# Folding the last quarter of W1 on the vector engine instead of the tensor engine, in a quaternion-conditioned feed-forward kernel

## The reference

```
xf = ifft(fft(x_quat, over tokens) * gate).real      # gate: one number a lane, so xf = x_quat * gate
q_l, q_r = cond / |cond|, q_right / |q_right|        # per lane (64 lanes)
z  = hamilton(q_l, hamilton(xf, conj(q_r)))          # cond and x: component by component, per lane
p  = softmax(z @ Wr.T)[:, 7]                         # 8 experts, the last one's probability
h  = gelu(z @ W1[7] + b1[7])                         # 256 -> 1024
out = x + (h @ W2[7] + b2[7]) * p                    # 1024 -> 256
```

## Time and profile before

| | |
|---|---|
| median of 3 runs | 105.12 us (105.01 to 106.14) |
| the profiled execution | 105.81 us, of which its span 104.0 us |
| granted TensorE clock | 1.0 (mean) |
| busy: TensorE, its loader | 100.2 us (96%), 84.9 us (82%) |
| busy: VectorE, ScalarE, GpSimd | 67.0 us (64%), 50.0 us (48%), 25.6 us (25%) |
| DMA | 8.38 MB, mean 81 GB/s |

### The profile page before, as it was taken

How to read it: one execution, slowest core, us unless ns; L and a number is a source line. 1 busy time by engine, 2 the same in 40 slices (tenths; PEclk the granted TensorE clock), 3 DMA queues, 4 the chain that set the end, 5 groups by cost and what they waited for, 6 DMA issues and landing times.

```text
span 104.0 us, 1512 instructions
## 1 busy us (share of the span) xinstructions
PE 100.2 (96%) x568; PEld 84.9 (82%) x568; DVE 67.0 (64%) x145; ACT 50.0 (48%) x83; POOL 25.6 (25%) x16
## 2 busy tenths in 40 slices
PE   7899999999999999999999999999999999999990
PEld 7779978888888888888888888888888878888980
DVE  1579689888274999298225996272494962378451
ACT  1466794544442484484414534944424544442700
POOL 3300000029999300000000000069998000000000
PEclk9999999999999999999999999999999999999999
DMA  3989990260004132450500050000005040000005
GB/s 67 319 266 343 261 121 0 50 135 22 0 3 158 44 115 93 94 111 0 202 0 0 0 208 0 0 0 0 0 0 202 6 202 0 0 0 0 0 7 195
DMA packets 10870, 8.38 MB, mean 81 GB/s; under 512 B 7920, under 2 KB 8816, under 8 KB 10864
## 3 DMA queue, kind: packets, MB, share of 16 engines
q1 hardware_dynamic: 10144, 7.51, 25.0%
q10 hardware_dynamic: 720, 0.79, 2.2%
HBM read 6.20 MB, written 2.10 MB: 80 GB/s over the span
## 4 chain that ended last, share of the span: by engine, by line
PE 93%; DMA 2%; DVE 2%; DVEq 0%; issue 0%
PE pre L690 40%; PE acc L697 26%; PE acc L705 15%; PE pre L654 3%; PE acc L606 2%; PE lT_bank L643 2%; DMA quats<-in_small 2%; PE acc L625 2%; PE acc L701 1%; PE acc L699 1%; DVE y L513 1%; PE lT_bank L625 1%; PE acc L616 0%; DVEq L73 0%; DVE R L390 0%
## 5 line engine op out<-in xcount | busy, mean ns | idle before, releaser
L341 ACT ACTIVATE h_hi<-pre,quats 128x512 fp32r<-128x512 f32 x32 | 22.1, 692 | 43.7 <-PE pre L690 41.8
L479 DVE TENSOR_TENSOR h_lo<-h_all,h_hi 128x512 fp32r<-128x512 f32 x32 | 21.8, 689 | 20.3 <-ACT h_all L343 20.1
L697 PE MATMUL acc<-w_parts,h_hi 128*128 128x512 f32 x116 | 32.4, 392 | 0.0
L697 PEld LDWEIGHTS acc<-w_parts,h_hi 128*128 128x128 f32 x116 | 21.5, 188 | 4.7 <-DVE w_lo L455 0.3
L690 PE MATMUL pre<-xT_hi,w_hi 128*128 128x512 f32 x60 | 24.0, 400 | 0.0
L690 PE MATMUL pre<-xT_lo,w_hi 128*128 128x512 f32 x60 | 23.6, 394 | 0.0
L705 PE MATMUL acc<-w_parts,h_lo 128*128 128x256 f32 x128 | 23.0, 282 | 0.0
L288 POOL TENSOR_TENSOR exps<-e_const,shifted 128x32 f32<-128x32 f32 x4 | 22.2, 5578 | 0.2
L705 PEld LDWEIGHTS acc<-w_parts,h_lo 128*128 128x128 f32 x128 | 20.0, 189 | 2.6 <-DVE h_lo L479 0.7
L343 ACT ACTIVATE h_all<-pre,quats 128x512 f32<-128x512 f32 x32 | 21.9, 684 | 0.0
L690 PE MATMUL pre<-xT_hi,w_lo 128*128 128x512 f32 x60 | 18.7, 392 | 0.0
(11 more groups left out here) (71 smaller groups left out, 61.2 us busy)
## 6 DMA issues: line engine op xcount, KB each, us to landing
x_sq<-in_x SPq DMA_DIRECT2D x12, 128.0 KB, 3.7
x_in<-in_x SPq DMA_DIRECT2D x3, 512.0 KB, 3.2
out<-y SPq DMA_DIRECT2D x3, 512.0 KB, 2.7
w<-in_W SPq DMA_DIRECT2D x4, 256.0 KB, 4.4
x_in<-in_x SPq DMA_DIRECT2D x2, 256.0 KB, 4.6
w_rest<-in_W_rest SPq DMA_DIRECT2D x2, 256.0 KB, 3.4
w_first<-in_W_first ACTq DMA_DIRECT2D x2, 132.0 KB, 2.8
x_sq<-in_x SPq DMA_DIRECT2D x4, 64.0 KB, 3.4
```

The costliest lines, as they stand in the source:

```text
L341: nc.scalar.activation(h_hi[:, s, :], pre_bank(b, f)[:, :], ACT.Gelu, bias=b1_cols[:, f:f + 1]).then_inc(h_hi_ready, 1)
L479: nc.vector.tensor_tensor(h_lo[:, s, :], h_all[:, s, :], h_hi[:, s, :].bitcast(F32), ALU.subtract).then_inc(h_lo_ready, 1)
L697: nc.tensor.matmul(acc[j][:, :], rows, w2_parts[:, f, :, :], start=(f == 0), stop=False)
```

## The change

TensorE no longer folds piece 3. The host gives the unfolded piece as before; the SP queue loads its four component groups of 32 rows one by one, and each goes to all four groups of 32 partitions (`w1_last`, four loads of 256 KB written). GpSimd computes the coefficients of M by column (`column_M`) from a new small input `columns` in five instructions. VectorE sums the four groups: `scale_last_w1` multiplies the first by its coefficient, `add_last_w1(o)` multiplies group o and adds it. Each is one instruction per half. ScalarE writes the high part (`last_w1_high`) behind its splits of x after f = 4, VectorE the low part (`last_w1_low`) behind the logits. The split of W2 piece 2 moves from after low_hidden 3 to behind that. In the SP queue the pieces 2 and 3 of W2, b2 and the second half of the first x move behind the squares of block 1.

```diff
@@ loads on the SP queue
-            for i in range(2, N_CHUNKS):
-                sp.dma_start(w1_rest[:, i - 1, :, :], W1_rest[i - 1]).then_inc(w1_loaded[i], 16)
-            for i in range(FT // W2_TILES):
...
-            sp.dma_start(b2_all[:, :], b2.to_broadcast([P, C])).then_inc(b2_loaded, 16)
-            sp.dma_start(x_in[:, TT // 2:TT, :], first_halves[1]).then_inc(first_x_loaded[1], 16)
+            sp.dma_start(w1_rest[:, 1, :, :], W1_rest[1]).then_inc(w1_loaded[2], 16)
...
+            def load_last_w1(o):
+
+                rows = W1_rest[N_CHUNKS - 2, o * SQ:(o + 1) * SQ, :, :].rearrange("l k f -> l (k f)")
+                sp.dma_start(w1_last[:, o, :, :], rows.unsqueeze(0).to_broadcast([QUADS, SQ, KC * CHUNK])
+                             ).then_inc(w1_last_loaded[o], 16)
+
+            sp.dma_start(column_quats[:, :], columns).then_inc(columns_loaded, 16)
+            load_w2(0)
+            load_last_w1(0)
+            load_last_w1(1)
+            load_w2(1)
+            load_last_w1(2)
+            load_last_w1(3)
             sp.wait_ge(x_turned, turned(0))
             load_squares(1)
+            load_w2(2)
+            load_w2(3)
+            sp.dma_start(b2_all[:, :], b2.to_broadcast([P, C])).then_inc(b2_loaded, 16)
+            sp.dma_start(x_in[:, TT // 2:TT, :], first_halves[1]).then_inc(first_x_loaded[1], 16)
@@ GpSimd, behind the inverse norms
+            pool.wait_ge(q_loaded, 16)
+            pool.wait_ge(columns_loaded, 16)
+            nc.gpsimd.tensor_tensor(column_signed[:, :, :], column_right,
+                                    column_signs.unsqueeze(1).to_broadcast([P, KC, 16]),
+                                    ALU.mult).then_inc(column_signed_ready, 1)
+            pool.wait_ge(column_signed_ready, 1)
+            for k in range(KC):
+                nc.gpsimd.tensor_tensor(column_terms[:, k, :, :], ..., ALU.mult).then_inc(column_terms_ready, 1)
+            pool.wait_ge(column_terms_ready, KC)
+            nc.gpsimd.tensor_tensor(column_pairs[:, :, :, :], column_terms[:, :, :, 0:2], column_terms[:, :, :, 2:4],
+                                    ALU.add).then_inc(column_pairs_ready, 1)
+            pool.wait_ge(column_pairs_ready, 1)
+            nc.gpsimd.tensor_tensor(column_M[:, :, :], column_pairs[:, :, :, 0], column_pairs[:, :, :, 1],
+                                    ALU.add).then_inc(column_M_ready, 1)
@@ ScalarE
+            def last_w1_high():
+                act.wait_ge(w1_last_added, 4 * KC)
+                nc.scalar.activation(w1_hi[:, :, chunk(3)], w1_last_sum[:, :, :], ACT.Copy).then_inc(w1_hi_ready, 1)
...
                     if b == 0 and f == 0:
                         split_w1(2)
-                        split_w1(3)
                     if f == 4 and b < LAST:
                         for k in range(KC):
                             split_x(b + 1, k)
+                        if b == 0:
+                            last_w1_high()
@@ VectorE
+            def scale_last_w1():
+
+                dve.wait_ge(column_M_ready, 1)
+                dve.wait_ge(w1_last_loaded[0], 16)
+                for k in range(KC):
+                    nc.vector.tensor_scalar(w1_last_sum[:, k, :], w1_last[:, 0, k, :], column_M[:, k, 0:1], None,
+                                            ALU.mult).then_inc(w1_last_added, 1)
+
+            def add_last_w1(o):
+
+                dve.wait_ge(w1_last_loaded[o], 16)
+                for k in range(KC):
+                    dve.wait_ge(w1_last_added, KC * (o - 1) + k + 1)
+                    nc.vector.scalar_tensor_tensor(
+                        out=w1_last_sum[:, k, :], in0=w1_last[:, o, k, :], scalar=column_M[:, k, o:o + 1],
+                        in1=w1_last_sum[:, k, :], op0=ALU.mult, op1=ALU.add).then_inc(w1_last_added, 1)
+
+            def last_w1_low():
+                dve.wait_ge(w1_hi_ready, 3)
+                nc.vector.tensor_tensor(w1_lo[:, :, chunk(3)], w1_last_sum[:, :, :], w1_hi[:, :, chunk(3)].bitcast(F32),
+                                        ALU.subtract).then_inc(w1_lo_ready, 1)
...
             split_w2(0)
+            scale_last_w1()
...
                     split_w1(2)
-                    split_w1(3)
+                    add_last_w1(1)
                 low_hidden(b, 1)
...
                 low_hidden(b, 3)
                 if b == 0:
-                    split_w2(2)
+                    add_last_w1(2)
+                    add_last_w1(3)
                 low_hidden(b, 4)
                 if b % 2 == 0:
                     logits_of(b // 2)
+                if b == 0:
+                    last_w1_low()
+                    split_w2(2)
@@ TensorE
             def fold(i):
                 pe.wait_ge(w1_loaded[i], 16)
-                if i == 3:
-
-                    pe.wait_ge(w1_lo_ready, 1)
...
                     if f == 0 and b == 0 and j == 3:
 
-                        pe.wait_ge(w1_lo_ready, N_CHUNKS - 1)
+                        pe.wait_ge(w1_lo_ready, 1)
...
             opening()
-            fold(3)
```

More of the change, by code:

```diff
@@ L36, in rotation_terms, with adaln_ffn @@
     return component, sign
-def adaln_ffn(nc, x, small, W1_first, W1_rest, W2, b2, out):
+def adaln_ffn(nc, x, small, columns, W1_first, W1_rest, W2, b2, out):
     n_batch, n_seq, C = x.shape
@@ L91, in adaln_ffn @@
         b1_cols = quats[:, AT_B1:]
+        column_quats = sb("column_quats", [P, KC * 16 + 16])
+        column_right = column_quats[:, 0:KC * 16].rearrange("p (k n) -> p k n", k=KC)
+        column_signs = column_quats[:, KC * 16:]
+        column_signed = sb("column_signed", [P, KC, 16])
+        column_terms = sb("column_terms", [P, KC, 4, 4])
+        column_pairs = sb("column_pairs", [P, KC, 4, 2])
+        column_M = sb("column_M", [P, KC, 4])
         squares = sb("squares", [P, KC, 2 + 1 + 4 + 1])
@@ L103, in adaln_ffn @@
         w1_first = sb("w1_first", [P, KC, CHUNK + NE])
-        w1_rest = sb("w1_rest", [P, N_CHUNKS - 1, KC, CHUNK])
+        w1_rest = sb("w1_rest", [P, N_CHUNKS - 2, KC, CHUNK])
+        w1_last = sb("w1_last", [P, 4, KC, CHUNK])
+        w1_last_sum = sb("w1_last_sum", [P, KC, CHUNK])
         b2_all = sb("b2_all", [P, C])
@@ L149, in adaln_ffn @@
         wr_ps = [bank[:, CHUNK:CHUNK + NE] for bank in acc[:KC]]
-        fold_banks = [None] + [bank[:, :].rearrange("p (k f) -> p k f", k=KC) for bank in (acc[3], lT_bank, acc[3])]
+        fold_banks = [None] + [bank[:, :].rearrange("p (k f) -> p k f", k=KC) for bank in (acc[3], lT_bank)]
         q_loaded = sem("q_loaded")
@@ L155, in adaln_ffn @@
         w1_first_loaded = [sem(f"w1_first_loaded{k}") for k in range(KC)]
-        w1_loaded = [None] + [sem(f"w1_loaded{i}") for i in range(1, N_CHUNKS)]
+        w1_loaded = [None] + [sem(f"w1_loaded{i}") for i in range(1, N_CHUNKS - 1)]
+        w1_last_loaded = [sem(f"w1_last_loaded{o}") for o in range(4)]
+        columns_loaded = sem("columns_loaded")
+        column_signed_ready = sem("column_signed_ready")
+        column_terms_ready = sem("column_terms_ready")
+        column_pairs_ready = sem("column_pairs_ready")
+        column_M_ready = sem("column_M_ready")
+        w1_last_added = sem("w1_last_added")
         w2_loaded = [sem(f"w2_loaded{i}") for i in range(FT // W2_TILES)]
@@ L233, in _, with load_w2 @@
                 sp.dma_start(x_sq[q * SQ:(q + 1) * SQ, 0:QUADS * TT // 2, :], first_squares[q]).then_inc(first_sq_loaded, 16)
-            for i in range(2, N_CHUNKS):
-                sp.dma_start(w1_rest[:, i - 1, :, :], W1_rest[i - 1]).then_inc(w1_loaded[i], 16)
-            for i in range(FT // W2_TILES):
+            sp.dma_start(w1_rest[:, 1, :, :], W1_rest[1]).then_inc(w1_loaded[2], 16)
+            def load_w2(i):
                 tiles = slice(i * W2_TILES, (i + 1) * W2_TILES)
                 sp.dma_start(w2[:, tiles, :], W2[i]).then_inc(w2_loaded[i], 16)
-            sp.dma_start(b2_all[:, :], b2.to_broadcast([P, C])).then_inc(b2_loaded, 16)
-            sp.dma_start(x_in[:, TT // 2:TT, :], first_halves[1]).then_inc(first_x_loaded[1], 16)
             def load_squares(b):
@@ L280, in _ @@
                                     ALU.pow).then_inc(inv_norms_ready, 1)
+            pool.wait_ge(q_loaded, 16)
[5 more added lines that the diff above has]
+            for k in range(KC):
+                nc.gpsimd.tensor_tensor(column_terms[:, k, :, :],
+                                        column_signed[:, k, :].rearrange("p (o t) -> p o t", t=4),
+                                        left_terms[:, k, :].unsqueeze(1).to_broadcast([P, 4, 4]),
+                                        ALU.mult).then_inc(column_terms_ready, 1)
+            pool.wait_ge(column_terms_ready, KC)
[4 more added lines that the diff above has]
+                                    ALU.add).then_inc(column_M_ready, 1)
             for pair in range(N_BLOCKS // 2):
@@ L793 @@
         [left[:, :, [0, 1, 1, 1]], right[:, :, component[o].reshape(16)], gate], axis=2) for o in range(n_quat)])
```

(3 more changed lines are left out.)

## The result

The changed kernel takes 113.6 us (median of 6 runs, 112.72 to 114.85), the kernel before 105.48 on the same chip (6 runs, 104.92 to 106.14): ratio 1.075, 95% interval 1.0673 to 1.0827. The prediction said 104.1, range 103.8 to 105.1, and gave "slower" 0.07. It was wrong in sign and by 9.5 us. The profiled span is 112.4 us, against 104.0.

What follows compares the result with a forecast made beforehand. The prediction took TensorE to bound the kernel, busy 100.2 of 104.0 us. Dropping fold(3) (0.86) and its wait (0.14) gave -1.00, other work was priced at 0: 105.12 - 1.00 = 104.1 us, range 103.8 to 105.1.

Steps and rivals of the forecast that it cites:

- Loads: SP queue: quarters land 0.8 us apart, squares when they did; reading the same rows four times costs 0.
- C: GpSimd's coefficients M come late and hold VectorE's scalings, or a broadcast quarter lands late there; up to 105.7 us; chance 0.08.
- -1.00 us on TensorE: TensorE's chain in block 0: fold(3) goes, 0.86 us, and the wait for VectorE before acc[3], 0.14 us.
- The adds at 0.40: VectorE's adding steps of 128x256 with two SBUF inputs take 0.40 us each.
- The two scalings: VectorE behind the split of W2 piece 0: 0.45 us together, in a gap, so they cost nothing.
- The place with the least to spare: End of block 0: low_hidden 7, reached through logits and exps, is over at 31.60; the weight loader wants it at 31.76.
- one for one: VectorE delay ahead of the logits beyond 0.16 us returns in full as a TensorE stall at the end of block 0.
- The 0.16 us to spare: Margin between low_hidden 7's end at 31.60 and the weight loader's due time of 31.76.
- Case B: VectorE's adds are slower than 0.40, six with 0.16 us more: 104.9 us, half of that 104.4; chance 0.15.
- Case D: VectorE is shut out while GpSimd runs the exps; TensorE stands some 4.0 us: 108.1 us; chance 0.01.

Runs made afterwards that it cites:

- copies4x32: Changed kernel with the host's four copies of each quarter and an unused row behind each 32, so 4 groups are outermost: 114.09 us, ratio 1.077.
- copies128: Changed kernel with each quarter of piece 3 stored four times by the host, so a load reads 128 different rows, 128 outermost: 104.74 us, ratio 0.9905.
- copies_between: copies128 with the squares of block 1 issued ahead of the last two quarters and nothing else changed: 104.41 us, ratio 0.9897.
- sixteen_loads: Changed kernel with each quarter loaded by four loads of 32 partitions, two quarters ahead of the squares and two behind: 104.54 us, ratio 0.9908.
- squares_between: Changed kernel with the squares of block 1 issued behind two quarters of piece 3 instead of four: 112.98 us, ratio 1.0681.
- early_logits: copies128 with the last adding step, piece 3's low part and W2 piece 2 behind the logits, squares ahead of the last two quarters: 104.95 us, ratio 0.9956.
- keep_busy29: Changed kernel with 29 matmuls on zeros where TensorE stands idle before the router of block 0: 112.93 us, ratio 1.0684.
- one_row: Changed kernel with each quarter's load giving one row to all 128 partitions, leaving wrong values in the last piece: 108.0 us, ratio 1.019.
- copies_inside: Changed kernel with 32 rows outermost and the four copies inside, leaving out the right row order of the last piece: 104.56 us, ratio 0.9917.

## Why the prediction was wrong

**The step that failed** is "Loads": "The broadcast reads the same HBM rows four times; b2's broadcast shows no price for it. Cost 0". The row it leaned on is a load of another shape: b2's broadcast has the 128 partitions outermost, this one has 4 copies. It cost 9.35 us (copies4x32 against copies128): 2.86 us from quarter to quarter where the prediction had 0.8, and the squares, issued behind them, landed at 24.9 where they were due at 16.7. What I had checked, bytes, size of the rows, number of issues and their place in the queue, was all right and did not decide. I had used the 340 GB/s of the earlier trace rows for a load of which no row had the shape, and set no upper bound on it, though the prediction bounded every other unknown price; at one quarter of the rate, 85 GB/s, the four quarters take 3.1 us each from 8.5 on, which puts the squares beyond 20 (an estimate) and would have given the loss its sign.

**The cases.** None held it. C was nearest, a quarter that lands late, but with 0.08 and at the scalings, where it was 1 us late and cost little. The main loss came from loads behind the broadcasts, which the change only moves; I had written that the squares land "when they did".

**What was right**, seen where the load is repaired: -1.00 us on TensorE (19.25 against 20.25). The time agrees too, 104.74 with ratio 0.9905 where 104.1 of 105.12 is 0.990, but the interval of that ratio is 0.3 us wide to either side, and the profiled execution had kept only 0.64 us of the gain and started 0.26 us ahead: that the number is so close is in part luck. The adds at 0.40 (measured 0.39). GpSimd was overpriced, 1.4 us for the five instructions instead of 2.7, so rival C in its first form never came near. The two scalings took 0.61 us together, not 0.45, inside a gap. The place with the least to spare, its due time and "one for one" were right (the table above). The 0.16 us to spare was too little for a VectorE that waits for nobody: copies_between and sixteen_loads show 0.40. In copies128 the squares took all of it and more. Even with 16 engines they landed at 17.26 us, and not "when they did". Case B did not happen. Case D did not either: in copies128 VectorE's conversion of W2 piece 2 took 0.52 us with GpSimd at work, against 0.42 without.

## What to carry to other kernels

Read a load's outermost dimension before its bytes: with 4 copies outermost it gets 4 of the 16 DMA engines, and what is issued behind it has its share on these four and is late with it. Put a dimension of the partitions outermost, split the load by partitions, or lay the copies out beforehand. When a price is taken from a row, compare the shape of the access too, and where none fits, let the bound reach to a multiple. After a repair, look at the next due time: in squares_between, early_logits and keep_busy29 moving the squares, moving the logits or holding the clock each uncovered the next wait. Measure a wait from a fixed point before it to the end of the work behind it, since the gap in the chain can be less than what it costs.

## What the runs showed of the hardware

- A DMA issue is not a fixed cost: an issue of the squares of block 1 took 0.57 to 1.0 us in the kernel before, up to 2.0 in copies128 and 1.2 to 3.7 us behind the four-engine loads, and it held up everything else on SyncE.
- Behind a wait TensorE loses more than the gap: the first matmul of tile 7 took 0.47 instead of 0.23 us in copies128.
- A 256 KB load of one HBM row to 128 partitions, on 16 engines, landed after 8.2 us in the median (one_row), of different rows after 5.8 (copies128), and with four reads of each row after 4.6 (copies_inside).
- The page's count of packets under 512 B tells how many engines a load used: 16 more for each load with 32 or 128 outermost, 4 more with 4.
- Four loads of 64 KB in place of one of 256 KB cost nothing that the time shows here, at 0.46 us of issue each (sixteen_loads).
- GpSimd's multiplications and additions on 8 to 32 elements a partition took 0.2 to 0.3 us each.
